# A Mamba block and a mixture of experts on one core: buffers, PSUM banks and an order of their own for the last group's eight expert pairs

## The chip, the cores and the metric

The kernel runs on one core of one Trainium2 chip. The metric is the device time of one execution in microseconds (us). Engines: PE (TensorE), DVE (VectorE), ACT (ScalarE), POOL (GpSimd), and SP, which here only issues DMAs ("SPq" in the trace).

## The reference, cut to what matters

All 32 sequences ("batches" below) of 512 tokens x 256 features, in float32:

```
h = x + mamba(layernorm(x))                      # scan over time, 512 channels x 16 states
x = layernorm(x + h + mlp(layernorm(h)))         # exact gelu
scores = softmax(x @ gate_w.T); top 2 of 8 experts per token
routed = sum over the two: weight * down_e(silu(gate_e(x)) * up_e(x))
shared = down_s(silu(gate_s(x)) * up_s(x))
out = layernorm(x + routed + shared)
```

## The kernel before, in words

**Batches.** Everything up to the routing is done batch by batch. DVE's time scan (`hs`, L1076) is done 64 times a batch; around it ACT forms decays (L655), POOL products `dBx` (L504), PE turns the states (L840) and DVE sums them (L1092).

**Groups.** Batches are collected in groups of 6, 6, 6, 6, 4, 2, 1 and 1. POOL scatters each token's row to two slots of `X_slots` in HBM (L536), sorted by expert. When a group's last batch is routed, DVE computes a table (`where`, `ends`; L1244 to L1273, semaphore `s_meta`): for every tile of 128 slots its first row and its expert. SP writes 128 rows of zeros behind each expert's rows (L406, "pads"), and then the tiles are worked on in pairs.

**A pair** `p` uses `xin[p % 2]`, `wx[p % 2]`, one `xsT`, one `ge` and one PSUM bank `psE`: SP loads two tiles of rows and their weights (L413 `wx`, L415 `xin`); PE transposes (L979, called T here); ACT copies to `xsT` (L739); PE multiplies by gate and up weights (L997, U); ACT tanh (L744), DVE twice (L1222, L1225) to `ge`; PE multiplies by down weights (L1012, D); ACT scales (L755, semaphore `s_yo`); SP stores to `Y_slots` (L431). T of pair p waits for `s_yo` of pair p-1, since `psE` is shared. The last group has eight pairs, 152 to 159.

**Finish.** For each batch f: SP loads `fx` (L444) after batch f-1 is stored, POOL adds the two gathered rows per token (L557, eight DMAs), DVE takes statistics (L1286), POOL the scale, ACT normalizes (L768) and stores `out`. There is one `fx`.

**Order.** Each engine's program is woven from strands (`scan`, `post`, `experts`, `results`, `finish`, ...). Each strand yields at its steps, and the table `AT` gives each step a due time in ticks (64 ticks a batch period); `weave` takes the earliest. Nothing is decided at run time: an engine's queue is this order, and each instruction waits on its semaphores with all behind it. `pairs_in` and `fins_in` say which pairs and finishes fall into which period.

Of the kernel before, what the change touches and what calls it, by code (L numbers as in the profile page):

```python
# [9 lines left out]
def group_sizes(n):  # L10
# [6 lines left out]
    while n:  # L17
# [21 lines left out]
    "ACT_weigh": [7.57, 8.5, 10.26, 11.55, 34.88, 35.01, 35.8, 36.57],  # L39
    "DVE_experts": [124.69, 126.85, 133.73, 139.5, 146.19, 149.9, 150.86, 154.7, 160.93, 165.34, 170.46, 174.99],  # L40
    "DVE_finish": [151.17, 151.17, 151.21, 152.66, 153.77, 171.26, 171.26, 171.41, 171.42, 171.42, 192.14, 192.26,
        193.44, 193.44, 193.44],
    "DVE_meta": [109.64, 109.93, 112.83, 112.83],
    "DVE_post": [59.72, 61.22, 67.08, 70.22, 72.85, 74.06, 75.11, 78.75, 84.22, 84.22, 85.78, 85.78, 85.78, 92.6,
        95.36, 97.26, 97.42, 98.01, 101.51, 103.99, 104.19, 104.25, 104.43, 105.16, 106.33, 108.33, 109.14, 109.14,
        109.97],
    "DVE_pre": [-60.86, -60.52, -60.52, -60.52, -45.76, -29.96, -29.11, -29, -28.49, -24.62, -24.37, -24.22, -22.6,
        -19.43, -18.25, -18.25, -18.11, -17.83, -17.83, -17.74, -17.48],
    "DVE_scan": [1.57, 2.09, 2.09, 2.36, 7.61, 7.63, 9.59, 9.96, 10.13, 11.26, 14.4, 15.73, 17.79, 19.19, 19.19,
# [4 lines left out]
    "DVE_weigh": [15.65, 17.23, 19.8, 20.31, 22.03, 22.04, 22.04, 22.04, 22.25, 22.25, 22.91, 23.69, 24.75, 24.95,  # L54
# [3 lines left out]
    "PE_experts": [123.37, 123.37, 126.75, 127.73, 131.97, 132.13, 138.88, 139.03, 140.94, 140.94, 146.68, 147.27,  # L58
        148.29, 148.29, 153.4, 153.97, 160.38, 160.38, 162.99, 163.09, 168.17, 168.35, 170.23, 170.23],
# [20 lines left out]
        62.82],  # L80
    "SP_B_rows": [-10.64],
    "SP_B_spread": [-7.66, -2.43, -1.84, 1.33, 4.3, 11.62, 24.83, 28.97, 32.58, 35.25, 35.45, 35.45, 43.34, 43.34,
        43.34, 43.34],
    "SP_behind": [0.69, 52.08, 55.74],
    "SP_experts": [110.32, 115.22, 124.29, 133.31, 141.52, 144.6, 147.29, 149.91, 155.71, 164.08, 168.27, 171.3],
    "SP_finish": [137.9, 162.22, 173.84],
# [23 lines left out]
def build(nc, a, out):  # L110
# [62 lines left out]
    with ctx:  # L173
# [1164 lines left out]
```

## Time and profile before

| | |
|---|---|
| median of 3 runs | 5640.32 us (5627.19 to 5643.27) |
| profiled execution | 5645.75 us, span 5644.0 us |
| busy share of the span | DVE 83%, PE 77%, POOL 64%, ACT 57% |
| granted PE clock, mean | 0.896 of full |

Busy shares are averages over a long part in which all engines work and an end in which few do. DVE's tenths in 40 slices of 141 us each read 8 and more up to slice 38, and 2 and 0 in the last two.

### The profile page before, as it was taken

The numbers are of one execution on the slowest core, as the hardware profiler recorded it, in microseconds if no ns is written. First come the engines' busy times: TensorE is split into PE (matmuls) and PEld (weight loads), VectorE is DVE, ScalarE is ACT, GpSimd is POOL, SyncE is SP. The second block draws the span as 40 slices with busy tenths as digits, with TensorE's granted clock in tenths as the row PEclk, the third lists the DMA queues.
The fourth block names the chain that finished last, engine by engine and source line by source line (L and its number), as shares of the span: only waits on it lengthen the run. The fifth ranks groups of instructions, "written<-read, shape, count | busy, mean of one in ns | idle before, by whom it ended". The sixth has DMA issues, their size and how long they took to land. (4 is left out here: it accounts for less than half of the span.)

```text
span 5644.0 us, 75862 instructions
## 1 busy us (share of the span) xinstructions
PE 4329.5 (77%) x20928; PEld 2991.4 (53%) x20928; DVE 4657.8 (83%) x7212; ACT 3195.6 (57%) x5088; POOL 3587.7 (64%) x2252
## 2 busy tenths in 40 slices
PE   4777777788778777777787887777788888887763
PEld 2454445555555555555555555555555555655542
DVE  6888888888888898888888888988988898888820
ACT  4555555555555556556665665665666565565521
POOL 4566666556555567666666766666677775777732
PEclk7888888898889999999999999999999999998885
DMA  1422222233333323332232333223244442555553
GB/s 62 107 78 79 77 72 75 75 105 104 113 113 95 114 85 98 95 101 87 80 91 77 102 93 101 86 76 97 77 120 122 121 116 81 146 151 138 156 136 94
DMA packets 357156, 563.53 MB, mean 100 GB/s; under 512 B 40433, under 2 KB 203378, under 8 KB 356610
## 3 DMA queue, kind: packets, MB, share of 16 engines
q1 hardware_dynamic: 253250, 398.07, 23.4%
q0 software_dynamic: 49152, 67.27, 5.8%
q10 hardware_dynamic: 54336, 93.34, 5.0%
q8 instruction: 174, 2.85, 0.2%
q14 instruction: 244, 2.00, 0.1%
HBM read 440.66 MB, written 186.05 MB: 111 GB/s over the span
## 5 line engine op out<-in xcount | busy, mean ns | idle before, releaser
L504 POOL TENSOR_TENSOR dBx<-dtx,Bbc 128x1024 f32<-128x1024 f32 x1024 | 2441.6, 2415 | 1011.4 <-DVE hs L1076 911.7
L1076 DVE TENSOR_TENSOR_SCAN hs<-ps,dBx 128x512 f32<-128x512 f32 x2048 | 2403.5, 1207 | 192.6 <-ACT ps L655 133.4
L655 ACT ACTIVATE ps<-dt,A 128x512 f32<-128x512 f32 x2048 | 1393.0, 690 | 829.8 <-DVE hs L1076 712.1
L840 PE MATMUL ps<-ident,hs 128*128 128x128 f32 x8192 | 1335.8, 303 | 418.3 <-DVE acc L1092 224.9
L840 PEld LDWEIGHTS ps<-ident,hs 128*128 128x128 f32 x8192 | 1030.3, 155 | 833.0 <-DVE acc L1092 456.5
L1092 DVE SCALAR_TENSOR_TENSOR acc<-ps,C_tok,acc 128x512 f32<-128x512 f32 x1792 | 1288.4, 739 | 191.1 <-PE ps L840 168.8
L805 PE MATMUL ps<-xnT,w_in 128*128 128x512 f32 x512 | 360.0, 842 | 273.4 <-DVE xc L1066 170.3
L557 POOL DMA_INDIRECT fx<-Y_slots,slots x256 | 405.2, 1583 | 210.1 <-DMA fx<-shared 131.4
L536 POOL DMA_INDIRECT X_slots<-xs,slots x256 | 256.6, 1002 | 385.3 <-DVE slots L1210 317.4
L1061 DVE SCALAR_TENSOR_TENSOR xc<-ps,conv_w,xc 128x511 f32<-128x511 f32 (+2 forms) x384 | 286.3, 746 | 178.0 <-ACT xc L615 170.9
L997 PE MATMUL ps<-xsT,wx 128*128 128x128 f32 x2560 | 353.2, 294 | 61.3 <-ACT xsT L739 61.3
L997 PEld LDWEIGHTS ps<-xsT,wx 128*128 128x128 f32 x2560 | 331.4, 207 | 94.0 <-issue 92.1
L805 PEld LDWEIGHTS ps<-xnT,w_in 128*128 128x128 f32 x512 | 118.6, 251 | 393.4 <-issue 306.1
L615 ACT ACTIVATE xc<-ps,conv_b,conv_w 128x512 f32<-128x512 f32 x128 | 99.4, 777 | 398.0 <-PE ps L805 385.7
L857 PE MATMUL ps<-xnT,w_in 128*128 128x512 f32 x512 | 275.6, 642 | 50.2 <-DVE post_tmp L1125 50.2
L1222 DVE SCALAR_TENSOR_TENSOR ge<-ge,ps 128x256 f32<-128x256 f32 x160 | 66.1, 413 | 248.7 <-ACT ge L744 248.4
L921 PE MATMUL ps<-w_m,post_tmp 128*128 128x256 f32 x1024 | 255.5, 380 | 0.0
L887 PE MATMUL ps<-w_out,xc 128*128 128x256 f32 x1024 | 255.3, 384 | 0.0
L904 PE MATMUL ps<-mT,w_m 128*128 128x512 f32 x512 | 237.5, 597 | 2.5 <-ACT mT L695 2.5
L739 ACT ACTIVATE xsT<-ps 128x512 f32<-128x512 f32 x160 | 95.3, 596 | 252.4 <-PE ps L979 237.9
L1012 PE MATMUL ps<-wx,ge 128*128 128x256 f32 x640 | 191.4, 426 | 46.3 <-DVE ge L1225 45.1
L979 PE MATMUL ps<-ident,xin 128*128 128x128 f32 x640 | 107.8, 295 | 152.7 <-DMA xin<-X_slots 144.4
(166 smaller groups left out, 6113.3 us busy)
## 6 DMA issues: line engine op xcount, KB each, us to landing
Bbc<-B_scratch SPq DMA_DIRECT2D x512, 256.0 KB
wx<-in_experts SPq DMA_DIRECT2D x320, 384.0 KB
Y_slots<-zeros ACTq DMA_DIRECT2D x228, 256.0 KB
xin<-X_slots SPq DMA_DIRECT2D x320, 128.5 KB
Y_slots<-xin SPq DMA_DIRECT2D x320, 128.0 KB
xt<-in_x SPq DMA_DIRECT2D x32, 512.0 KB, 5.4
shared<-xt ACTq DMA_DIRECT2D x32, 512.0 KB
fx<-shared SPq DMA_DIRECT2D x32, 512.0 KB, 3.6
```

The source lines that it names most:

```text
L504: pool.tensor_tensor(dBx[u % 3][:], dtx[b % 2][:, 2 * h:2 * h + 2, :], Bbc[g % NBB][:, n % CH:n % CH + 1, :].broadcast_to([P, 2, T]), ALU. ...
L536: pool.indirect_dma_start(out=X_slots[g % 2], out_offset=bass.IndirectOffsetOnAxis(ap=slots[:, b % NKEPT, c, t:t + 1], axis=0), in_=xs[:, ...
L557: pool.indirect_dma_start(out=fx[:, t, :], out_offset=None, in_=Y_slots[g % 2], in_offset=bass.IndirectOffsetOnAxis(ap=slots[:, f % NKEPT, ...
L655: act.activation(psA[s % 2][:], dt[b % 2][:, j, :], ACT.Exp, scale=A[:, j, n:n + 1]).then_inc(s_dA, 1)
L805: i = pe.matmul(bank(b, j)[:], w_in[:, k, j * P:(j + 1) * P], xn[:, k, :], start=(k == 0), stop=(k == KD - 1))
L840: i = pe.transpose(psH[w % 2][:, j * P:(j + 1) * P], hs[(n * CT + j) % NHB][:, t * P:(t + 1) * P], ident[:])
L857: i = pe.matmul(psG[j % 2][:], w_in[:, k, DI + j * P:DI + (j + 1) * P], xn[:, k, :], start=(k == 0), stop=(k == KD - 1))
L921: i = pe.matmul(psG[q][:, t * D:(t + 1) * D], post_tmp[:, k, (2 * q + t) * P:(2 * q + t + 1) * P], w_m2[:, k, :], start=False, stop=(k == ...
L997: i = pe.matmul(psE[:, o * HALF + m * P:o * HALF + (m + 1) * P], w[:, m, (2 * k + o) * P:(2 * k + o + 1) * P], xsT[:, (m * KD + k) * P:(m ...
L1061: dve.scalar_tensor_tensor(out=c[:, j, s:], in0=bank(b, j)[:, 0:T - s], scalar=conv_w[:, j, NK - 1 - s:NK - s], in1=c[:, j, s:], op0=ALU.m ...
L1076: dve.tensor_tensor_scan(hs[s % NHB][:], psA[s % 2][:], dBx[s // 2 % 3][:, s % 2, :], 0.0, ALU.mult, ALU.add).then_inc(s_scan, 1)
L1092: dve.scalar_tensor_tensor(out=o, in0=psH[w % 2][:], scalar=C_tok[b % 2][:, t, n:n + 1], in1=o, op0=ALU.mult, op1=ALU.add).then_inc(s_weig ...
```

## The change

The eight pairs of the last group leave the strands `experts` and `results` and get a strand `last` on each of SP, PE, ACT and DVE, placed at the end of period 31. They use eight weight tiles, eight row tiles, eight `xsT`, and eight halves of `Bbc` as `ge`, all laid over buffers that the scan has left, and six PSUM banks in turn. On PE the steps of three pairs alternate: D of pair q-2, U of pair q-1, T of pair q. SP issues the pads as soon as the table is there, without waiting for the scatter, then all weights, then all rows, then all stores. The function `pad` is also used for the other groups, where `all_rows` follows at once. `fins_in` no longer counts the last group by its pairs. The table `AT` has new numbers for nearly every entry of all strands; one line of it stands at the diff's end. In the diff the first `last` is SP's and the second PE's; ACT's has the same order of steps, and DVE's goes pair by pair. The lines of POOL are from its `finish`.

```diff
-        g = sum(first[g] + groups[g] - 1 <= b for g in range(NG))
+        g = min(sum(first[g] + groups[g] - 1 <= b for g in range(NG)), NG - 1)
         waiting = pairs_to[g - 1] - ended
-        left = groups[g] - (b - first[g] + 1) if g < NG else 1
+        left = max(groups[g] - (b - first[g] + 1), 1)
         take = min(waiting, PAIRS_MAX, -(-waiting // left))
-        ready = sum(groups[g] for g in range(NG) if pairs_to[g] <= ended)
+        ready = sum(groups[g] for g in range(NG - 1) if pairs_to[g] <= ended) + (groups[NG - 1] if b >= NB else 0)
...
+    P0, NLAST = pairs_to[NG - 2], tiles[NG - 1] // 2
...
+        wx_last = [wx[P0 % 2], wx[(P0 + 1) % 2]] + [pair_of(v[:]) for v in (dt[0], dt[1], dtx[0], dtx[1], xc[o], acc[z])]
+        xin_last = [xin[P0 % 2], xin[(P0 + 1) % 2]] + [rows_of(v[:]) for v in (*dBx, xnT[o], xt[NB % NX_IN], xt[(NB + 1) % NX_IN])]
+        xsT_last, ge_last = hs[0:NLAST], [Bbc[q // 2][:, 0, q % 2 * HALF:(q % 2 + 1) * HALF] for q in range(NLAST)]
+        ps_last = [psE, psP, *psA, *psH]
...
+            def pad(g):
+                sp.wait_ge(s_meta, (g + 1) * NMETA)
...
+                for e in range(NE):
+                    r = sp.value_load(ends[g % 2][0:1, e:e + 1], min_val=0, max_val=ROWS - P)
+                    sp.dma_start(X_slots[g % 2][bass.ds(r, P), :], zeros[:, 0:ROW]).then_inc(s_padded[g % 2], 16)
+
+            def all_rows(g):
+                sp.wait_ge(s_scattered, (first[g] + groups[g]) * 2 * NTB * 16)
+                sp.wait_ge(s_padded[g % 2], (g // 2 + 1) * NE * 16)
+
+            def last():
+                g, b = NG - 1, NB - 1
+                for q in range(NLAST):
+                    yield b
+                    if q == 0:
+                        pad(g)
+                        sp.wait_ge(s_scan, NB * STEPS)
+                        sp.wait_ge(s_y_turned, NB * CT)
+                    if q < 2:
+                        sp.wait_ge(s_down_e, P0 - 1 + q)
+                    for i in range(2):
+                        e = sp.value_load(where[g % 2][0:1, 1, 2 * q + i:2 * q + i + 1], min_val=0, max_val=NE * P)
+                        sp.dma_start(wx_last[q][:, i, :], a["experts"].rearrange("e p f -> (e p) f")[
+                            bass.ds(e, P), :]).then_inc(s_wx_last[q], 16)
+                for q in range(NLAST):
+                    yield b
+                    if q == 0:
+                        all_rows(g)
+                        sp.wait_ge(s_kept, (NB - 1) * 16)
+                    if q < 2:
+                        sp.wait_ge(s_Y_out[(P0 + q) % 2], stores(P0 - 2 + q, (P0 + q) % 2))
+                    for i in range(2):
+                        r = sp.value_load(where[g % 2][0:1, 0, 2 * q + i:2 * q + i + 1], min_val=0, max_val=ROWS - P)
+                        sp.dma_start(xin_last[q][:, i, :], X_slots[g % 2][bass.ds(r, P), :]).then_inc(s_xin_last[q], 16)
+                for q in range(NLAST):
+                    yield b
...
+                    sp.wait_ge(s_yo_last, (q + 1) * 2)
...
+                        sp.dma_start(Y_slots[g % 2][bass.ds(r, P), :], xin_last[q][:, i, 0:D]).then_inc(s_Y_last, 16)
...
+            def last():
+                for s_ in range(NLAST + 2):
+                    for q, step in ((s_ - 2, 2), (s_ - 1, 1), (s_, 0)):
+                        if not 0 <= q < NLAST:
+                            continue
+                        bank_, w = ps_last[q % NPS], wx_last[q]
+                        yield NB - 1
+                        if step == 0:
...
+                            if q >= NPS:
+                                pe.wait_ge(s_yo_last, (q - NPS + 1) * 2)
+                            pe.wait_ge(s_xin_last[q], 32)
...
+                            i.then_inc(s_turned_last, 1)
+                        elif step == 1:
+                            pe.wait_ge(s_wx_last[q], 32)
+                            pe.wait_ge(s_xsT_last, q + 1)
...
+                            i.then_inc(s_up_last, 1)
+                        else:
+                            pe.wait_ge(s_hidden_last, q + 1)
...
+                            i.then_inc(s_down_last, 1)
...
                                 if (c, t) == (0, 0):
                                     pool.wait_ge(s_fx_in, 16 * (f + 1))
-                                    for k in range(2):
-                                        pool.wait_ge(s_Y_out[k], stores(pairs_to[g] - 1, k))
+                                    if g == NG - 1:
+                                        pool.wait_ge(s_Y_last, NLAST * 32)
+                                    else:
+                                        for k in range(2):
+                                            pool.wait_ge(s_Y_out[k], stores(pairs_to[g] - 1, k))
...
-    "DVE_weigh": [15.65, 17.23, 19.8, 20.31, 22.03, 22.04, 22.04, 22.04, 22.25, 22.25, 22.91, 23.69, 24.75, 24.95,
+    "DVE_weigh": [15.5, 17.23, 21.12, 21.12, 21.68, 21.68, 22.06, 22.22, 22.66, 22.81, 22.91, 23.41, 24.71, 24.91,
```

SP's queue at the end of the program, before: from the last group's last pad to its first row load. `TENSOR_LOAD` and `ISA` are the reads of the table.

```order
L406 DMA X_slots1<-zeros 128x257
L411 TENSOR_LOAD where1
L411 ISA x2
L412 TENSOR_LOAD where1
L412 ISA x2
L413 ISA
L413 DMA wx0<-in_experts 128x768
L415 ISA
L415 DMA xin0<-X_slots1 128x257
```

The same place after the change:

```order
L426 DMA X_slots1<-zeros 128x257
L444 TENSOR_LOAD where1
L444 ISA x2
L445 ISA
L445 DMA wx0<-in_experts 128x768
L444 TENSOR_LOAD where1
L444 ISA x2
L445 ISA
L445 DMA wx0<-in_experts 128x768
```

Behind the pads a weight load was followed by its row load; now it is followed by the next weight load, and fourteen more, before the first row load. And further down in the same queue, at the rows of the last group's third and fourth pair (`dBx0` and `dBx1` lie under them), after the change:

```order
L456 DMA dBx0<-X_slots1 128x257
L455 TENSOR_LOAD where1
L455 ISA x2
L456 ISA
L456 DMA dBx0<-X_slots1 128x257
L514 DMA fx<-shared 128x1024
L455 TENSOR_LOAD where1
L455 ISA x2
L456 ISA
L456 DMA dBx1<-X_slots1 128x257
```

Batch 30's `fx` load stands between the third and the fourth pair's rows, as it did before, but the stores of the first two pairs, which stood ahead of it, now stand behind all row loads.

PE's queue at the last group, before:

```order
L979 MATMUL ps5<-ident,xin0 128x128 x4
L997 MATMUL ps5<-xsT,wx0 128x128 x8
L1012 MATMUL ps5<-wx0,ge 128x256 x2
L979 MATMUL ps5<-ident,xin1 128x128 x4
L997 MATMUL ps5<-xsT,wx1 128x128 x8
L1012 MATMUL ps5<-wx1,ge 128x256 x2
```

PE's queue at the same place, after (T L1128, U L1137, D L1145; the `hs` tiles are `xsT`, the `Bbc` tiles `ge`):

```order
L1128 MATMUL ps5<-ident,xin0 128x128 x4
L1137 MATMUL ps5<-hs0,wx0 128x128 x8
L1128 MATMUL ps4<-ident,xin1 128x128 x4
L1145 MATMUL ps5<-wx0,Bbc0 128x256 x2
L1137 MATMUL ps4<-hs1,wx1 128x128 x8
L1128 MATMUL ps0<-ident,dBx0 128x128 x4
L1145 MATMUL ps4<-wx1,Bbc0 128x256 x2
L1137 MATMUL ps0<-hs2,dt0 128x128 x8
```

Between U and D of one pair there is now T of the next, and T of a pair stands two places ahead of its U.

On DVE the statistics of batch 29 (L1429 after the change) stand ahead of the first pair's step and those of batch 30 between the seventh pair's and the eighth's; on ACT batch 30's normalizing stands ahead of the eighth pair's tanh.

DVE's queue in the middle of the program (batch 15, `hs` the scan, `acc` the sums), before:

```order
L1092 SCALAR_TENSOR_TENSOR acc1<-ps3,C_tok1,acc1 128x512
L1076 SCALAR_TENSOR_TENSOR hs4<-ps0,dBx2 128x512
L1092 SCALAR_TENSOR_TENSOR acc1<-ps2,C_tok1,acc1 128x512
L1092 SCALAR_TENSOR_TENSOR acc1<-ps3,C_tok1,acc1 128x512
L1076 SCALAR_TENSOR_TENSOR hs5<-ps1,dBx2 128x512
L1076 SCALAR_TENSOR_TENSOR hs6<-ps0,dBx0 128x512
L1076 SCALAR_TENSOR_TENSOR hs7<-ps1,dBx0 128x512
```

The same place after:

```order
L1225 SCALAR_TENSOR_TENSOR acc1<-ps3,C_tok1,acc1 128x512
L1209 SCALAR_TENSOR_TENSOR hs4<-ps0,dBx2 128x512
L1225 SCALAR_TENSOR_TENSOR acc1<-ps2,C_tok1,acc1 128x512
L1209 SCALAR_TENSOR_TENSOR hs5<-ps1,dBx2 128x512
L1225 SCALAR_TENSOR_TENSOR acc1<-ps3,C_tok1,acc1 128x512
L1209 SCALAR_TENSOR_TENSOR hs6<-ps0,dBx0 128x512
L1209 SCALAR_TENSOR_TENSOR hs7<-ps1,dBx0 128x512
```

The second and third sum of the piece stood together, and now a scan step stands between them; in most places of the long part the two orders differ by as little.

## Rows read from the trace of the kernel before

**Rows 1.** Busy time by stretch, the long part: start:end, length, engines, clock, DMA share, GB/s.

```profile
core 0: us, PE busy (x) PEld busy (x) DVE busy (x) ACT busy (x) POOL busy (x), PEclk, DMA share, GB/s
500.00:5300.00 4800.00, 3821.03 (x18765) 2647.02 (x18765) 4159.24 (x6325) 2852.33 (x4544) 3179.27 (x1942) 0.92 0.34 100
5200.00:5250.00 50.00, 44.31 (x269) 35.57 (x270) 40.49 (x60) 30.31 (x53) 32.24 (x21) 1.00 0.65 177
```

**Rows 2.** Shares kept, one a batch (L727), and the two most frequent kinds of wait, 500 to 5300.

```profile
L727 ACTq DMA_DIRECT2D shared<-xt x32: 326/331/366, 324.7 to 5469.7; - x32
...
POOL dBx L504 <- DVE hs L1076: 798.2, 330, 10.6
...
DVE acc L1092 <- PE ps L840: 153.0, 250, 3.7
```

**Rows 3.** Busy time by stretch of 10 us in the end, columns as above.

```profile
5460.00:5470.00 10.00, 5.58 (x28) 3.90 (x26) 7.55 (x33) 3.88 (x8) 6.09 (x8) 1.00 0.22 79
5480.00:5490.00 10.00, 0.00 (x0) 0.00 (x0) 0.00 (x0) 0.00 (x0) 4.77 (x4) 0.50 0.80 144
5490.00:5500.00 10.00, 0.00 (x0) 0.00 (x0) 0.00 (x0) 0.00 (x0) 6.06 (x4) 0.50 0.78 175
5500.00:5510.00 10.00, 6.95 (x24) 5.38 (x24) 0.84 (x2) 1.15 (x3) 0.00 (x0) 0.50 0.32 103
5560.00:5570.00 10.00, 6.20 (x25) 5.11 (x26) 2.53 (x10) 1.82 (x4) 0.47 (x2) 0.67 0.34 108
```

**Rows 4.** Instructions in order of time, SP's DMAs at the last group's start.

```profile
5470.43 0.21 DVE L1273 SCALAR_TENSOR_TENSOR where<-few 1x56 int32<-1x56 f32 x1
...
5470.72 0.38 ACTq L771 DMA_DIRECT2D out<-fx  x1
...
5473.99 0.33 SPq L444 DMA_DIRECT2D fx<-shared  x1
...
5478.28 1.63 POOL L557 DMA_INDIRECT fx<-Y_slots,slots  x1 [2.43 <-DMA fx<-shared]
5479.56 9.82 SPq L406 DMA_DIRECT2D X_slots<-zeros  x8
...
5489.87 1.54 POOL L557 DMA_INDIRECT fx<-Y_slots,slots  x1 [4.41 <-DMA fx<-Y_slots,slots]
...
5493.40 0.36 SPq L413 DMA_DIRECT2D wx<-in_experts  x1
...
5495.43 1.55 POOL L557 DMA_INDIRECT fx<-Y_slots,slots  x1 [0.30 <-issue]
5495.61 0.33 SPq L413 DMA_DIRECT2D wx<-in_experts  x1
5496.13 0.33 SPq L415 DMA_DIRECT2D xin<-X_slots  x1
...
5500.69 1.12 PE L979 MATMUL ps<-ident,xin 128*128 128x128 f32 x4 [31.66 <-DMA xin<-X_slots]
```

**Rows 5.** The last pair, in order of time: T, xsT, U, D, scaling, then batch 31's load.

```profile
5599.67 1.09 PE L979 MATMUL ps<-ident,xin 128*128 128x128 f32 x4 [1.02 <-ACT xin L755]
...
5601.53 3.75 PE L997 MATMUL ps<-xsT,wx 128*128 128x128 f32 x16 [0.78 <-ACT xsT L739]
...
5606.68 2.08 PE L1012 MATMUL ps<-wx,ge 128*128 128x256 f32 x4 [1.39 <-DVE ge L1225]
5608.79 0.84 ACT L755 ACTIVATE xin<-ps,xin 128x256 f32<-128x256 f32 x2 [3.08 <-PE ps L1012]
5611.89 0.37 SPq L444 DMA_DIRECT2D fx<-shared  x1
```

**Rows 6.** A pair of the group before, in order of time, PE alone: T, U, D.

```profile
5454.49 0.60 PE L979 MATMUL ps<-ident,xin 128*128 128x128 f32 x4
5455.86 2.02 PE L997 MATMUL ps<-xsT,wx 128*128 128x128 f32 x16 [0.78 <-ACT xsT L739]
5459.27 1.13 PE L1012 MATMUL ps<-wx,ge 128*128 128x256 f32 x4 [1.38 <-DVE ge L1225]
```

**Rows 7.** Batch 29's finish, in order of time: statistics, normalizing, store.

```profile
5517.68 1.40 DVE L1286 BATCH_NORM_STATS2 stats_fin<-fx 128x6 f32<-128x256 f32 x4
...
5521.57 2.07 ACT L768 ACTIVATE fx<-fx,nb_fin,rs_fin 128x256 f32<-128x256 f32 x4 [0.80 <-POOL nb_fin L570]
5523.67 0.38 ACTq L771 DMA_DIRECT2D out<-fx  x1
```

**Rows 8.** The page, DMA queues: packets, MB, share of 16 engines over the span.

```profile
q1 hardware_dynamic: 253250, 398.07, 23.4%
```

More of the change, by code:

```diff
@@ new lines @@
+    "POOL_pre": [-47.46, 1.12, 3.62],
+    "POOL_scan": [1.53, 3.89, 8.19, 8.19, 8.84, 8.84, 12.39, 14.56, 17.84, 21.37, 24.69, 24.69, 26.76, 29.36, 29.36,
+        29.75, 30.39, 30.39, 31.18, 32.15, 32.15, 32.65, 32.65, 37.83, 42.18, 44.28, 44.81, 45.74, 55.56, 55.72,
+        56.44, 63.18],
+    "SP_B_rows": [-9.09],
+    "SP_B_spread": [-3.46, -2.29, -2.27, 11.26, 17.49, 19.82, 19.82, 19.82, 28.51, 28.51, 28.51, 30.14, 36.45, 39.06,
+        44.23, 44.23],
+    "SP_behind": [27.68, 83.6, 93.32],
@@ L270, in build @@
         s_xin, s_wx, s_Y_out = [[sem(f"{n}{i}") for i in range(2)] for n in ("xin", "wx", "Y_out")]
+        s_wx_last, s_xin_last = [[sem(f"{n}_last{q}") for q in range(NLAST)] for n in ("wx", "xin")]
+        s_Y_last = sem("Y_last")
         s_B_in = [sem(f"B_in{i}") for i in range(NBB)]
@@ L300, in build @@
                                                                             "down_e")]
+        s_turned_last, s_xsT_last, s_up_last, s_tanh_last = [sem(n + "_last") for n in ("turned", "xsT", "up", "tanh")]
+        s_silu_last, s_hidden_last, s_down_last, s_yo_last = [sem(n + "_last") for n in ("silu", "hidden", "down", "yo")]
         NROUTE, NMETA = 21, 18
@@ new lines, in all_rows @@
+            def all_rows(g):
[27 more added lines that the diff above has]
+                    yield b
+                    if q == 0:
+                        sp.wait_ge(s_gathered, gathers(first[before[g]] + groups[before[g]] - 1))
+                    sp.wait_ge(s_yo_last, (q + 1) * 2)
+                    for i in range(2):
+                        r = sp.value_load(where[g % 2][0:1, 0, 2 * q + i:2 * q + i + 1], min_val=0, max_val=ROWS - P)
+                        sp.dma_start(Y_slots[g % 2][bass.ds(r, P), :], xin_last[q][:, i, 0:D]).then_inc(s_Y_last, 16)
@@ L396, in experts @@
                         yield b
-                        sp.wait_ge(s_meta, (g + 1) * NMETA)
-                        sp.wait_ge(s_scattered, (first[g] + groups[g]) * 2 * NTB * 16)
                         if tile == 0:
-                            if g < 2:
-                                sp.wait_ge(s_Y_cleared[g], CLEARS * 16)
-                                sp.wait_ge(s_zeros, 16)
-                                sp.wait_ge(s_behind, 32)
-                            for e in range(NE):
-                                r = sp.value_load(ends[g % 2][0:1, e:e + 1], min_val=0, max_val=ROWS - P)
-                                sp.dma_start(X_slots[g % 2][bass.ds(r, P), :], zeros[:, 0:ROW]).then_inc(s_padded[g % 2], 16)
-                            sp.wait_ge(s_padded[g % 2], (g // 2 + 1) * NE * 16)
+                            pad(g)
+                            all_rows(g)
                         if p >= 2:
@@ L447, in _ @@
                   (experts(), AT["SP_experts"]),
-                  (results(), AT["SP_results"]), (finish(), AT["SP_finish"]))
+                  (results(), AT["SP_results"]), (finish(), AT["SP_finish"]), (last(), AT["SP_last"]))
             sp.wait_ge(s_stored, 16 * NB)
@@ L774, in _ @@
                   (post(), AT["ACT_post"]), (experts(), AT["ACT_experts"]), (results(), AT["ACT_results"]),
-                  (finish(), AT["ACT_finish"]), (clear(), AT["ACT_clear"]))
+                  (finish(), AT["ACT_finish"]), (clear(), AT["ACT_clear"]), (last(), AT["ACT_last"]))
             act.wait_ge(s_stored, 16 * NB)
@@ L1016, in _ @@
             weave((turn(), AT["PE_turn"]), (pre(), AT["PE_pre"]), (post(), AT["PE_post"]), (inputs(), AT["PE_inputs"]),
-                  (experts(), AT["PE_experts"]), (results(), AT["PE_results"]))
+                  (experts(), AT["PE_experts"]), (results(), AT["PE_results"]), (last(), AT["PE_last"]))
         @block.vector
@@ L1225, in experts, with last @@
                         dve.tensor_tensor(ge[:], ge[:], psE[:, HALF:T], ALU.mult).then_inc(s_hidden_e, 1)
+            def last():
+                for q in range(NLAST):
+                    bank_ = ps_last[q % NPS]
+                    yield NB - 1
+                    dve.wait_ge(s_tanh_last, q + 1)
+                    dve.scalar_tensor_tensor(out=ge_last[q], in0=ge_last[q], scalar=1.0, in1=bank_[:, 0:HALF], op0=ALU.add,
+                                             op1=ALU.mult).then_inc(s_silu_last, 1)
+                    dve.wait_ge(s_silu_last, q + 1)
+                    dve.tensor_tensor(ge_last[q], ge_last[q], bank_[:, HALF:T], ALU.mult).then_inc(s_hidden_last, 1)
             def meta():
```

148 lines of the change are left out of this document (97 added, 51 removed), and 30 rows, old and new, of the table AT.

## The prediction

> **What bounds the kernel now.** I read the busy time by stretch first. From 500 to 5300 us DVE is busy 4159 of 4800 us, 87%, and PE 80% [rows 1]: both hold each other up, and a batch takes (5469.7 - 324.7) / 31 = 166.0 us [rows 2]. The reader should see that this part is one thing and the end another. From 5470 on the stretches are nearly empty: PE does nothing from 5480 to 5500, DVE under 1 us in the 10 us after [rows 3]. So the last 170 us are bound by a chain of waits, and that is where the change works.
>
> The instructions in order of time show that chain. The table is there at 5470.6 (5470.43 + 0.21), the pads are issued from 5479.56 to 5489.38, the first weights at 5493.40, and PE starts T of the first pair at 5500.69, having waited 31.66 us [rows 4]. The last pair's scaling ends at 5608.79 + 0.84 = 5609.6 [rows 5]. The eight pairs thus take 5609.6 - 5500.7 = 108.9 us, 13.6 each. A pair alone is 5609.6 - 5599.7 = 9.9 us [rows 5]; the rest is waiting for loads that may only be issued when the stores of the pair two before have landed, because there are two sets of tiles. Behind the last pair come stores, batch 31's load, gathers and normalizing: 5644.0 - 5609.6 = 34.4 us.
>
> **The change part by part.** I follow the same chain with the new queues.
>
> *Start of SP's work.* The pads no longer wait for the scatter but stand behind batch 29's `fx` load, which goes out at 5473.99, 3.3 us after batch 28's store was issued at 5470.72 [rows 4]. On ACT that store now stands ahead of the second half of the shared expert's last copy, which I estimate at 1.9 us earlier (three steps of 0.6 us): `fx` at 5472.1, and the first pad a table read behind it at 5473.2. The eight pads span 9.8 us [rows 4], so they end at 5483.
>
> *Sixteen weight loads.* One tile's two table reads and two issues took 5495.61 - 5493.40 = 2.2 us [rows 4], so 1.1 us each: sixteen take 17.6 us, and the first row load would go out at 5502. But the transfers are 16 x 128 x 768 x 4 bytes = 6.29 MB. SP's and ACT's queue q1 moved 398.07 MB in 23.4% of the span, which is 398.07 / (0.234 x 5644) = 301 GB/s at full share [rows 8]; at some 270, since gathers run beside it, the weights take 23.3 us and are in at about 5508. The rows queue behind. A row load took 5500.69 - 5496.13 = 4.6 us to T with traffic around it [rows 4]. I take T of the first pair at **5511**. Bounds: 5506 if only the issues count (two row issues and 2 to 3 us of landing), and 5531 if the rate is the 144 GB/s of 5480 to 5490 [rows 3], where 6.29 MB take 44 us. I am near the first because that row is full of small packets of gathers and weights are long ones. Against before this is +10.3 us: the early pads win 6 us, and fourteen weight loads ahead of the first rows lose more.
>
> The Trainium skill, "DMA: Bandwidth & Descriptors", section "Queues, rings and completion order", says that each DMA engine consumes one issuer's descriptors in ring order and takes turns between issuers packet by packet. By that rule the first rows do wait for all weights, which speaks against the change and for 5511 rather than 5506; the sum would be 5 us lower without it.
>
> *The pairs.* In the new order D of pair q-2, U of q-1, T of q follow each other on PE. From U's end to D's start are 1.39 us (tanh, two DVE steps) [rows 5], and T of the next pair lies within. The `xsT` copy lies beside D, the scaling beside U, the loads are ahead. What repeats is U + 1.39 + D. At half clock that is 3.75 + 1.39 + 2.08 = 7.22 us [rows 5]; at full clock 2.02 + 1.38 + 1.13 = 4.53 us [rows 6].
>
> Which clock? It stood at 1.00 up to 5470 and at 0.50, that is 1.2 GHz, from 5480 on, after PE had gone idle; with 6.95 busy of 10 us and holes between pairs it stayed at 0.50; in one stretch, with 6.20, it was 0.67 on average, so it rose and fell again [rows 3]. Where PE was busy 44.3 of 50 us it was 1.00 [rows 1]. In the new order PE is busy 6.9 of 7.22 us at half clock, and (0.60 + 2.02 + 1.13) / 4.53 = 83% at full clock, which is closer to the second of these. I take two pairs at half clock and six at full.
>
> The Trainium skill, "TensorE: Matmul & The Clock Gate", Part 1, says the same in general: half rate is the default and sustained activity releases it. By that rule the sum is the one I take; by the half-clock rows around the place it would be 13 us more.
>
> Sum: T and `xsT` of the first pair 1.09 + 0.78 = 1.9; two pairs 14.4; six pairs 27.2; last scaling 0.9; together 44.4 us.
>
> *Batch 30's finish* now stands in the middle of it: its statistics come before the eighth pair's DVE steps, and ACT's normalizing before the eighth tanh. From statistics to the end of normalizing took 5521.57 + 2.07 - 5517.68 = 6.0 us [rows 7]. In that time D and U of the full-clock pairs take 3.2 us, so the eighth tanh is 2.8 us late. Pair block: **47.2 us**, from 5511 to 5558.2.
>
> *Two waits hidden.* SP's queue holds batch 30's `fx` load between the third and fourth pair's rows, until batch 29 is stored. Its gathers ran from 5478.28 to 5497 with 4.4 us of waiting between the halves [rows 4]; landing (4), statistics and normalizing (6.0) and the store (3.3) give about 5509, and 5517 if the weights' traffic doubles the landing times. T of the fourth pair is due at 5511 + 1.9 + 14.4 + 2.0 = 5529, and needs its rows issued by 5524. So the wait is covered by 7 to 15 us; beyond that it costs its own length. The sixteen stores go at 1.1 us each, 2.2 a pair against 4.5, so SP keeps up. Batch 30 itself: load 4, gathers 15 + 4.4 + 4, ready at 5536 to 5544; its statistics are due at 5549. Hidden.
>
> *The end* behind the last scaling keeps its shape: 34.4 us.
>
> *The new order table* in the long part: the same work, in places one instruction earlier or later. DVE is idle 13% of 166 us, so there is something to win or lose. One typical wait of DVE is 153.0 / 250 = 0.6 us [rows 2]. One more or one less a batch is 0.6 x 31 = 19 us. I take 0, since nothing in the orders favours a side.
>
> Sum in the profile's time: +10.3 (start) + 47.2 - 108.9 (pairs) = -51.4; span 5644.0 - 51.4 = 5592.6, and the execution 5645.75 - 51.4 = 5594.4. The profiled execution is 5.4 us above the median of the runs, so I say **5589 us**.
>
> **The rivals.**
> 1. *The clock stays at half.* For it: it did so in every pair from 5500 to 5560 [rows 3]. Against: those had holes. Six periods cost 2.69 us more, less the 2.8 us that batch 30 then no longer costs: +13, 5602 us.
> 2. *The weights come slowly*, at 144 GB/s [rows 3]: T at 5531, +20, 5609 us.
> 3. *SP stands at batch 30's load.* If batch 29's gathers, statistics or store are late beyond 5524, the fourth pair's rows are late by as much. With 10 us, 5599 us.
> 4. *The new order costs more than the end gives* (the other side). The mechanism: POOL may write `dBx` only when DVE's scan has used it, a wait of 798.2 / 330 = 2.4 us on average [rows 2]; if the new order adds one a batch that DVE then feels, that is 75 us: 5664 us, slower. It decides from 51.4 / 31 = 1.7 us a batch on. For it: nearly every due time changed, in queues without slack. Against: in the orders neighbours swap places, no more.
>
> **How the numbers follow.** A change within 0.3% (17 us) can't be told from none: the limits are 5623 and 5657. Forecast 0.48, clock 0.17, weights 0.12, SP 0.07, new order 0.16. Faster: the first four, 0.84, less a little of their overlap with small losses in the long part, 0.83. Of the fourth rival's 0.16, 0.10 lie within the limits (1.1 to 2.2 us a batch) and 0.07, with what was taken off, above. The range: from 5589 down 19 (one wait less a batch) and 5 (issue-bound start), 5565; up 13 (clock) and 19 (one wait more), 5621, which takes in rivals 1 to 3 and leaves out rival 4. Rounded outward: 5563 to 5622.
>
> **What would show it.** T of the first pair some 40 us after batch 28's store, later than before by 10; PE's D, U, T with no hole but 1.4 us, the granted clock at 1.00 from the third pair on; the last scaling 34 us ahead of the end; 166.0 us a batch unchanged. It would be wrong if a batch's time moved by 1 us, if PE's waits at the rows came back behind the `fx` load, or if PE waited for weights.

## The result and the profile after

| | before | after |
|---|---|---|
| median | 5639.85 us (4 runs, 5627.19 to 5643.27) | 5446.44 us (4 runs, 5429.85 to 5454.42) |
| profiled execution, span | 5645.75, 5644.0 us | 5454.42, 5452.7 us |
| first and last share copy | 324.7, 5469.7 us | 316.7, 5335.8 us |
| a batch between them | 166.0 us | 161.9 us |
| last share copy to the end | 174.3 us | 116.9 us |

The ratio is 0.9657, with a 95% interval of 0.9627 to 0.9687: 193 us faster, where 51 were forecast. The busy time of the engines is nearly what it was, on a shorter span. Part 1 of the changed kernel's page:

```profile
PE 4290.8 (79%) x20928; PEld 2976.0 (55%) x20928; DVE 4632.5 (85%) x7212; ACT 3190.3 (59%) x5088; POOL 3587.7 (66%) x2252
```

The line with one entry a batch, the copies into `shared`, cuts the time in two, and that cut is the main reading of this case. In the columns of [rows 2]:

```profile
L800 ACTq DMA_DIRECT2D shared<-xt x32: 326/331/366, 316.7 to 5335.8; - x32
```

From the first copy to the last are 31 batches: (5335.8 - 316.7) / 31 = 161.9 us against 166.0. The first copy itself comes 8.0 us earlier. So the last copy comes 133.9 us earlier than before, and the end behind it is 174.3 - 116.9 = 57.4 us shorter. 133.9 + 57.4 = 191.3, which is the difference of the spans. The end is where the prediction looked; the long part was taken at nothing. The long part by stretch, in the columns of [rows 1]:

```profile
500.00:5300.00 4800.00, 3904.73 (x19256) 2720.82 (x19254) 4196.02 (x6458) 2881.76 (x4613) 3232.72 (x1989) 0.91 0.36 104
```

DVE is busy 4196 of 4800 us, 87.4% against 86.7%. Between the first copy and the last, DVE's waits for other engines fall from 21.6 to 18.3 us a batch and its busy time from 142.1 to 141.3 us. The shorter batch is thus in the main less waiting between the same instructions.

**The end**, in stretches of 10 us, answers to [rows 3]:

```profile
5350.00:5360.00 10.00, 0.00 (x0) 0.00 (x0) 0.00 (x0) 0.00 (x0) 3.56 (x3) 0.50 0.99 300
5360.00:5370.00 10.00, 0.00 (x0) 0.00 (x0) 0.52 (x2) 0.00 (x0) 3.07 (x2) 0.50 1.07 325
5370.00:5380.00 10.00, 4.32 (x19) 3.98 (x20) 1.27 (x7) 2.67 (x5) 1.71 (x4) 0.50 0.69 238
5380.00:5390.00 10.00, 7.94 (x55) 7.00 (x54) 2.11 (x5) 4.44 (x10) 6.32 (x4) 0.95 0.79 183
5390.00:5400.00 10.00, 7.60 (x52) 6.85 (x53) 2.11 (x5) 3.83 (x9) 6.21 (x4) 1.00 0.71 156
```

The weights move at 300 and 325 GB/s (all the core's transfers together, batch 29's gathers among them) with PE idle. PE starts in the stretch from 5370, and the clock is at 0.95 in the next and at 1.00 in the one behind it. The instructions in order of time, answering to [rows 4]:

```profile
5338.75 10.17 SPq L426 DMA_DIRECT2D X_slots<-zeros  x8
...
5349.81 3.67 SPq L445 DMA_DIRECT2D wx<-in_experts  x4
...
5365.43 1.42 SPq L445 DMA_DIRECT2D acc<-in_experts  x2
5367.74 3.97 SPq L456 DMA_DIRECT2D xin<-X_slots  x4
...
5374.90 1.09 PE L1128 MATMUL ps<-ident,xin 128*128 128x128 f32 x4 [39.77 <-DMA xin<-X_slots]
...
5378.46 0.33 SPq L514 DMA_DIRECT2D fx<-shared  x1
```

The pads start 3.0 us behind the last share copy (5335.80), where they were 9.9 behind it before; the sixteen weight loads take from 5349.81 to 5366.85, the first rows go out at 5367.74, and T is at 5374.90. The `fx` load of batch 30 waits until 5378.46 between the third and the fourth pair's rows, and PE has no wait on it. The same view a little later shows D (L1145) of two pairs in a row, and then the eighth pair's tanh, D and scaling behind batch 30's normalizing:

```profile
5386.20 1.13 PE L1145 MATMUL ps<-wx,Bbc 128*128 128x256 f32 x4 [0.95 <-DVE Bbc L1368]
...
5390.50 1.13 PE L1145 MATMUL ps<-dt,Bbc 128*128 128x256 f32 x4 [0.95 <-DVE Bbc L1368]
...
5411.47 2.07 ACT L863 ACTIVATE fx<-fx,nb_fin,rs_fin 128x256 f32<-128x256 f32 x4 [1.76 <-POOL nb_fin L643]
...
5414.00 0.38 ACT L845 ACTIVATE Bbc<-ps 128x256 f32<-128x256 f32 x1 [0.46 <-ACT fx L863]
...
5415.34 2.07 PE L1145 MATMUL ps<-acc,Bbc 128*128 128x256 f32 x4 [4.73 <-DVE Bbc L1368]
5417.46 0.84 ACT L850 ACTIVATE xt<-ps,xt 128x256 f32<-128x256 f32 x2 [3.08 <-PE ps L1145]
```

D to D is 5390.50 - 5386.20 = 4.30 us, with the next pair's U and the one's after it T between them. The eighth tanh (L845) comes at 5414.00, behind the normalizing (L863). PE has idled 4.73 us by the eighth D, which then takes 2.07 us instead of 1.13, the half-clock duration [rows 5]. Behind the same hole it took 1.47 us in the experiment late_pads below.

### The profile page after: what moved, and what is told of

It reads as the page before. It is cut to its first block and busy times, and to the rows that moved or that the text cites. A ratio compares the mean times of both kernels' runs of the same rounds, so it can differ in the third digit from the quotient of the medians.

```text
span 5452.7 us, 75679 instructions
## 1 busy us (share of the span) xinstructions
PE 4290.8 (79%) x20928; PEld 2976.0 (55%) x20928; DVE 4632.5 (85%) x7212; ACT 3190.3 (59%) x5088; POOL 3587.7 (66%) x2252
## 3 DMA queue, kind: packets, MB, share of 16 engines
q1 hardware_dynamic: 253250, 398.07, 24.2%
## 5 line engine op out<-in xcount | busy, mean ns | idle before, releaser
L935 PE MATMUL ps<-ident,hs 128*128 128x128 f32 x8192 | 1350.3, 305 | 486.2 <-DVE acc L1225 285.5
L900 PE MATMUL ps<-xnT,w_in 128*128 128x512 f32 x512 | 324.9, 762 | 178.8 <-DVE xc L1199 170.3
L1092 PE MATMUL ps<-xsT,wx 128*128 128x128 f32 x2432 | 318.6, 286 | 39.0 <-ACT xsT L812 38.7
L1092 PEld LDWEIGHTS ps<-xsT,wx 128*128 128x128 f32 x2432 | 303.3, 201 | 74.7 <-issue 74.2
L952 PE MATMUL ps<-xnT,w_in 128*128 128x512 f32 x512 | 279.2, 685 | 0.0
L900 PEld LDWEIGHTS ps<-xnT,w_in 128*128 128x128 f32 x512 | 108.9, 235 | 271.5 <-issue 267.7
L812 ACT ACTIVATE xsT<-ps 128x512 f32<-128x512 f32 x152 | 90.0, 592 | 212.8 <-PE ps L1074 211.8
L1107 PE MATMUL ps<-wx,ge 128*128 128x256 f32 x608 | 176.7, 416 | 45.6 <-DVE ge L1358 42.9
L1016 PEld LDWEIGHTS ps<-w_m,post_tmp 128*128 128x128 f32 x1024 | 189.8, 190 | 36.7 <-issue 14.4
L982 PEld LDWEIGHTS ps<-w_out,xc 128*128 128x128 f32 x1024 | 193.2, 190 | 25.6
```

Source lines behind the costliest of these rows:

```text
L900: i = pe.matmul(bank(b, j)[:], w_in[:, k, j * P:(j + 1) * P], xn[:, k, :], start=(k == 0), stop=(k == KD - 1))
L935: i = pe.transpose(psH[w % 2][:, j * P:(j + 1) * P], hs[(n * CT + j) % NHB][:, t * P:(t + 1) * P], ident[:])
L952: i = pe.matmul(psG[j % 2][:], w_in[:, k, DI + j * P:DI + (j + 1) * P], xn[:, k, :], start=(k == 0), stop=(k == KD - 1))
L982: i = pe.matmul(psG[q][:, t * D:(t + 1) * D], c[:, k, (2 * q + t) * P:(2 * q + t + 1) * P], w_out[:, k, :], start=False, stop=(k == CT - 1))
L1016: i = pe.matmul(psG[q][:, t * D:(t + 1) * D], post_tmp[:, k, (2 * q + t) * P:(2 * q + t + 1) * P], w_m2[:, k, :], start=False, stop=(k == ...
L1092: i = pe.matmul(psE[:, o * HALF + m * P:o * HALF + (m + 1) * P], w[:, m, (2 * k + o) * P:(2 * k + o + 1) * P], xsT[:, (m * KD + k) * P:(m ...
```

## The experiments

Fifteen further kernels were built from the two: the same code with other due times, or one edit of the last group's strand. Besides the ratio, each row gives the two parts from its profiled execution. The kernel before ran beside each of them, with medians of 5625.6 to 5642.5 us; gains and losses in us below are against the one beside the kernel. Since the kernels ran in several rounds, two of them are compared by their ratios and not by their medians. The two parts rest on one execution each. How much they vary without a cause can be seen in the long part: after, seq_last, late_pads and rows_early have the same code and order there, and their last share copies come at 5335.8, 5315.9, 5334.0 and 5309.2 us.

| kernel | median us | ratio to before, 95% | a batch | end part |
|---|---|---|---|---|
| code_only | 5575.7 | 0.988 (0.9849 to 0.991) | 165.6 | 118.7 |
| table_only | 5515.9 | 0.9792 (0.9763 to 0.9821) | 161.8 | 174.2 |
| new_act | 5578.0 | 0.989 (0.9855 to 0.9925) | 164.2 | 170.2 |
| new_pe | 5761.8 | 1.0214 (1.0185 to 1.0243) | 169.8 | 175.0 |
| act_pe | 5639.8 | 0.9995 (0.997 to 1.002) | 165.3 | 170.7 |
| act_dve | 5684.0 | 1.0101 (1.008 to 1.0122) | 167.9 | 167.3 |
| act_pe_dve | 5497.1 | 0.9779 (0.9758 to 0.98) | 161.4 | 170.5 |
| old_sp | 5481.7 | 0.9744 (0.9726 to 0.9763) | 161.1 | 174.0 |
| pre_act | 5636.8 | 1.0018 (0.9998 to 1.0039) | 165.5 | 173.4 |
| act_notpre | 5874.7 | 1.0436 (1.0406 to 1.0466) | 173.3 | 171.5 |
| seq_last | 5449.1 | 0.9667 (0.9639 to 0.9695) | 161.3 | 127.9 |
| late_pads | 5448.0 | 0.9657 (0.9632 to 0.9682) | 161.7 | 121.7 |
| rows_early | 5430.3 | 0.9629 (0.9599 to 0.966) | 161.0 | 115.4 |
| after_old_sp | 5419.7 | 0.9617 (0.9593 to 0.9641) | 161.0 | 115.8 |
| best | 5401.9 | 0.959 (0.9568 to 0.9612) | 160.5 | 112.0 |

### Code and table apart

code_only is the changed code with the old numbers for all 32 old strands; the strands `last` keep theirs, ACT's 0.75 later (134.91 for 134.16, and so on). The edit of one old strand:

```diff
-    "SP_behind": [27.68, 83.6, 93.32],
+    "SP_behind": [0.69, 52.08, 55.74],
...
```

> The new code of the last group with the old order table (ACT's steps of the new strand 0.75 tick later, so that batch 29's normalizing still stands ahead of them). Theory A, the gain has two sources, the end (57 us from batch 31's last share copy to the end: 174.3 before, 116.9 after) and the order table (134 us ahead of it): about 5640 - 57 = 5583 us, a batch at 166.0 us. Theory B, the table matters only together with the code (the function pad, the finishes that no longer count the last group): near 5446 us, a batch at 162 us.

table_only is the old code with the new numbers.

> The old code with the new order table. Theory A: 5640 - 134 = 5506 us, a batch at 161.9 us, the end as before (174 us). Theory B: near 5640 us.

Theory A held on both sides: 5575.7 and 5515.9 us, and the product of the ratios, 0.988 x 0.9792 = 0.9675, is the change's 0.9657 within the intervals. The code acts on the end part alone (118.7 us; a batch 165.6 against 166.0, the last copy 12 us earlier, inside the spread above), the table on the batches alone (161.8 us, end 174.2).

### Which engine's order

Each engine's queue depends only on its own engine's numbers, so the table can be divided by engine without any other effect. In these the old code got new numbers for all strands of the engines named. One strand's first line, for new_pe:

```diff
-    "PE_turn": [4.33, 4.9, 8.45, 9.97, 12.05, 12.46, 12.62, 13.39, 19.52, 19.52, 19.73, 20.13, 20.28, 20.28, 21.11,
+    "PE_turn": [4.62, 5.23, 8.11, 8.57, 12.27, 12.27, 12.73, 13.29, 19.39, 19.64, 19.73, 20.13, 20.28, 20.28, 21.11,
...
```

> The old code with the new order on PE alone. Theory A1, the gain is in the input convolution (DVE's waits for ACT's first tap fell from 143 to 58 us, ACT's waits for PE's input product from 349 to 220 us) and comes from PE's order, which brings those products earlier: 5510 to 5570 us. Theory A2, it comes from DVE's order, which puts the taps later: 5625 to 5655 us here.

> The old code with the new order on ACT alone. Theory A1 (PE's order) and A2 (DVE's order) both: 5620 to 5655 us. Theory A3, ACT's order lets the first tap go out earlier: 5510 to 5590 us.

> The old code with the new order on ACT and DVE. With ACT's alone DVE's waits for ACT's decays rose from 103 to 172 us; with all engines they are 77 us. Theory C1, DVE's new order takes those waits back: 5515 to 5545 us. Rival C2, DVE's order fits PE's new one only (PE's alone cost 119 us): slower than 5578 us.

> The old code with the new order on ACT and PE. So far: ACT alone 65 us faster, PE alone 119 slower, ACT and DVE 58 slower, all three 128 faster. Theory D1, the three orders are one schedule, and any two of them make the third wait: slower than 5640 us, with DVE's waits for PE's second MLP product (143 us with PE alone, 21 with all three) at 100 us or more. Rival D2, ACT's and PE's orders are the gain and DVE's is neutral: 5500 to 5530 us.

> The old code with the new order on ACT, PE and DVE, but POOL's and SP's as before. Theory C1 and C2 both: most of the 127 us, 5515 to 5535 us. Rival C3, the rest of the gain lies with the loads of Bbc and with POOL (POOL's waits for Bbc fell from 89 to 27 us): 5550 us or more.

ACT alone gains 65 us (A3's range), PE alone loses 119 (A1 and A2 are out), ACT with PE is nothing (D2 is out, and D1 too: the kernel was not slower, and the wait for the second MLP product, 100 us or more by D1, was 0.3 us), ACT with DVE loses 58 (C1 is out, C2 foretold it), and the three together gain 128 (C3 is out; the others' range is missed by 18 us on the fast side). What stands is C2: DVE's new order fits PE's. Beside ACT's alone it costs 123 us (from 65 gained to 58 lost), beside ACT's and PE's it brings 128. DVE alone and PE with DVE were not tried. So the gain belongs to no engine. The simplest view is DVE's waits in the first five batches after the first share copy, which hold no expert pairs. Before (us in total, times, longest):

```profile
DVE xc L1061 <- ACT xc L615: 24.8, 15, 3.1
DVE acc L1092 <- PE ps L840: 24.0, 41, 2.5
DVE hs L1076 <- ACT ps L655: 16.0, 15, 1.7
```

With the three new orders (other line numbers for the same instructions; L1027 is the first tap, L1042 the scan, L1058 the sum):

```profile
DVE acc L1058 <- PE ps L806: 18.6, 46, 1.3
DVE hs L1042 <- ACT ps L621: 12.1, 10, 1.5
DVE xc L1027 <- ACT xc L581: 10.5, 11, 1.7
```

All of DVE's waits there are 15.6 us a batch before and 9.7 after, and a batch is 156.0 and 150.0 us: the same 6 us. Over all 31 batches, with the whole new table (table_only), DVE's waits fall from 21.6 to 18.1 us a batch and its busy time from 142.1 to 141.3, together what a batch gained (166.0 to 161.8). In the first five batches with PE's new order alone they are 17.8, and a batch is 157.7:

```profile
DVE acc L1058 <- PE ps L806: 26.0, 46, 1.9
DVE stats_post L1068 <- PE ps L887: 25.3, 5, 5.6
...
DVE xc L1027 <- ACT xc L581: 13.9, 10, 2.1
```

The taps' wait fell here as well, but a wait that did not exist before stands beside it: `stats_post` (L1102 before), 25.3 us in five batches, for PE's second MLP product. By the numbers of the table, one more group of the scan's transposes stands ahead of the last of these products in PE's new order, and in DVE's new order one more sum stands ahead of the statistics that need it. With all three new orders the wait is gone in these batches. But it is gone with ACT's and PE's alone too, where DVE's order is the old one, and there another has grown, the scan's for PE (3.3 us before):

```profile
DVE acc L1058 <- PE ps L806: 23.6, 40, 1.8
DVE hs L1042 <- PE ps L806: 20.7, 10, 2.1
```

That is the coupling: a step moved on one engine saves a wait and makes another, and which one is made depends on the orders of two other engines. Which moves in the table bring the gain is not shown.

The same is seen inside one engine:

> The old code and order, with the new due times of ACT's strand pre alone (normalizing, first taps, tanh, the dt steps). With ACT's whole new order the kernel took 5578 us against 5643, and DVE's waits for ACT's first tap fell from 143 to 55 us. Theory A3, the moved taps are the source: 5570 to 5590 us, the waits for the tap as low. Rival, it is the places of ACT's scan steps and its other strands around the taps: 5630 to 5650 us.

> The old code and order, with the new due times of ACT's strands except pre. All of ACT's new due times gave 65 us, pre's alone nothing, although its waits for the tap fell. Theory M1, the gain of ACT's order is in its scan, post and expert steps: 5570 to 5590 us. Rival M2, it needs both parts: 5625 to 5650 us.

A3 fell with pre_act (5636.8 us, in its rival's range). M1 fell with act_notpre, and M2 was right that both parts are needed but missed the size: `pre` alone gives nothing and the rest of ACT alone costs 241 us (173.3 us a batch), yet the two together give 65. I had read the fall of one row as the cause. From 500 to 5300 us, before and then with ACT's new `pre`:

```profile
DVE xc L1061 <- ACT xc L615: 143.1, 83, 3.4
DVE hs L1076 <- ACT ps L655: 102.9, 106, 4.1
DVE ge L1222 <- ACT ge L744: 84.3, 53, 8.9
```

```profile
DVE acc L1058 <- PE ps L806: 188.5, 262, 3.7
DVE hs L1042 <- ACT ps L621: 130.7, 201, 3.9
DVE ge L1188 <- ACT ge L710: 97.7, 75, 8.1
DVE xc L1027 <- ACT xc L581: 60.3, 54, 3.1
```

The taps' wait (L1061, now L1027) falls from 143.1 to 60.3 us, and three others rise: sums 153.0 [rows 2] to 188.5, scan 102.9 to 130.7, `ge` 84.3 to 97.7. All of DVE's waits are 21.6 us a batch before and 21.2 with the new `pre`. The wait moved.

> The old code with the new order on all engines but SP, to be compared with 5516 us (new order on all). Theory C3: the late Bbc loads come back, POOL's waits for them rise from 41 to 80 us or more and the time to 5540 us or more. Theory C1: within 10 us of 5516.

C3 is refuted: the waits for `Bbc` did come back (POOL waited 93 us instead of 41 from 500 to 5300), and the kernel was not slower. The medians differ by 34 us in its favour, but they are of different rounds; by the ratios (0.9744 and 0.9792, intervals that just touch) it is some 27 us, and by the spans of the profiles 22, so C1's "within 10 us" was missed too. In this pair of profiles the last four batches took 170.6 us each against 176.8, which is 25 us. That SP's new order costs was tested again in the changed kernel:

> The changed kernel with the old due times for SP's old strands. With the old code, SP's old order beside the new order of the others took 5482 us against 5516 with all new, and the last four batches 170.6 us each against 176.8. Theory S1, SP's new order alone costs some 20 us: 5420 to 5430 us, the last four batches near 171. Rival S2, that was a difference of two runs of the old code only: 5440 to 5450 us.

```diff
-    "SP_behind": [27.68, 83.6, 93.32],
+    "SP_behind": [0.69, 52.08, 55.74],
...
```

SP's six other old strands got their old numbers in the same way. The median is 5419.7 us, at the edge of S1's range, but the intervals of the two ratios overlap, and part of these 27 us is spread. The last four batches decide it: 169.9 us each here and 169.9 in the kernel best below, with SP's old numbers, against 173.3, 173.5, 174.2 and 172.7 in after, seq_last, late_pads and rows_early, with its new ones. So S1 held in kind. SP's new order costs 3 to 4 us in each of the last four batches, some 14 us in all; the rest of the 27 is not shown to come from it. Which SP strand costs it stays open.

### The end part

```diff
-                for s_ in range(NLAST + 2):
-                    for q, step in ((s_ - 2, 2), (s_ - 1, 1), (s_, 0)):
+                for s_ in range(NLAST):
+                    for q, step in ((s_, 0), (s_, 1), (s_, 2)):
```

> The changed kernel, but on PE and ACT each of the eight pairs is done to its end before the next begins; tiles, banks and loads as changed. Theory T1, what the end gained is mostly that no pair waits for its loads, and the interleaving adds 1.6 us a pair at full clock (5.9 against 4.3): 5446 + 13 = 5459 us. Rival T2, the holes bring the clock back to half, 9.1 us a pair: 5446 + 34 = 5480 us.

By the ratios (0.9667 and 0.9657) the interleaving can't be told from nothing; by the end part of the profiled executions it is 127.9 - 116.9 = 11 us, near T1's 13. The long part was 20 us shorter in this kernel's profile, with the same code and order, so the end part is the sharper measure. The instructions in order of time bear it out: from the first T to the last scaling's end are 5409.44 - 5353.61 = 55.8 us here and 43.4 after the change, 12.4 longer; T came 1.4 us earlier, and behind the last scaling both have 34.4 us. PE alone, one pair and the next T:

```profile
5376.57 0.60 PE L1091 MATMUL ps<-ident,dBx 128*128 128x128 f32 x4
5378.24 2.02 PE L1100 MATMUL ps<-hs,dt 128*128 128x128 f32 x16 [1.07 <-ACT hs L804]
5381.65 1.13 PE L1108 MATMUL ps<-dt,Bbc 128*128 128x256 f32 x4 [1.38 <-DVE Bbc L1331]
5382.61 0.60 PE L1091 MATMUL ps<-ident,dBx 128*128 128x128 f32 x4
```

T to T is 6.04 us at full clock (T1: 5.9). T2 fell: with holes of 1.07 and 1.38 us the clock stays up, at 1.00 from 5370 to 5400.

```diff
                     if q == 0:
+                        sp.wait_ge(s_scattered, (first[g] + groups[g]) * 2 * NTB * 16)
                         pad(g)
```

> The changed kernel, but SP waits for the scatter before the last group's pads, as before. The pads began 4 to 5 us before the scatter landed, and all else on SP stands behind them: T of the first pair 5 us later, 5451 us. Rival: the first rows wait for the weights' transfers, which ran at 300 to 325 GB/s and start as much later, so that it is the same 5 us; if the gathers of batch 29 get through better in the meantime, 5446 us.

The end part grew by 121.7 - 116.9 = 4.8 us, as expected: T came 44.6 us behind the last share copy instead of 39.1, and the pairs took 42.8 us instead of 43.4. The ratios (0.9657 both) can't show it.

```diff
-                for q in range(NLAST):
+                def weights(q):
...
-                for q in range(NLAST):
+                def rows(q):
...
+                yield from weights(0)
+                for q in range(NLAST):
+                    if q + 1 < NLAST:
+                        yield from weights(q + 1)
+                    yield from rows(q)
```

> The changed kernel, but SP issues the weights of two pairs, then the rows of the first, and so on in turn, instead of all sixteen weight loads ahead of the first rows. Theory E1: T of the first pair comes 17 us earlier (at 22 instead of 39 us behind the last share copy), but batch 30's finish, which was ready only 4 us before its place, then sets the end: 5446 - 7 = 5439 us. Rival E2, the end follows the pairs: 5430 us. Rival E3, the transfers are the bound and nothing moves: 5446 us.

The median was 5430.3 us, which is E2's number, but by luck: the end part only went from 116.9 to 115.4 us, where E2 had 16 us less and E1 had 7. The rest is the long part, which has the same code and order as after and was 26.6 us shorter in this profile. T came earlier as said, at 5333.4, 24.2 us behind the share copy (5309.2) instead of 39.1. Then, in order of time:

```profile
5346.10 2.07 ACT L834 ACTIVATE fx<-fx,nb_fin,rs_fin 128x256 f32<-128x256 f32 x4 [36.92 <-POOL nb_fin L614]
...
5348.63 0.60 ACT L812 ACTIVATE hs<-ps 128x512 f32<-128x512 f32 x1 [0.46 <-ACT fx L834]
...
5349.37 3.76 PE L1108 MATMUL ps<-hs,wx 128*128 128x128 f32 x16 [14.87 <-ACT hs L812]
```

U waits 14.87 us, because on ACT the copy to `xsT` (L812) stands behind batch 29's normalizing (L834), which is not ready. E1 is right that the finishes are the bound, but it is batch 29's that meets the pairs first, and it takes nearly all of the gain. The run also shows what the late T was made of: in the changed kernel the first row load went out 31.9 us behind the last share copy, after 17 us of issuing weight loads, and T followed it by 7.2 us (5374.90 - 5367.74); here T followed the first row load by 4.9 us. Of the 14.9 us between the two, 12.6 are thus SP's issuing and 2.3 the way from there to T, which the weights ahead of the rows can have made longer.

```diff
-    "DVE_last": [135.94, 138.39, 138.39, 140.22, 147.13, 147.13, 147.78, 191.48],
+    "DVE_last": [126.0, 126.0, 138.39, 140.22, 147.13, 147.13, 147.78, 191.48],
...
```

> The changed kernel with SP's old due times, the rows issued in turn with the weights, the first pairs' ACT and DVE steps ahead of batch 29's finish, and the eighth tanh ahead of batch 30's normalizing. Theory E1 (the chain of finishes through the one fx tile sets the end once the pairs are early): from the last share copy to the end 111 us against 116.9 after the change, 5446 - 20 - 6 = 5420 us. Rival E2, the pairs set it: the end follows them by their 15 us, 102 us and 5411 us.

E1 held for the end part, 112.0 us against its 111. The total of 5401.9 us, the fastest version, is 18 us below E1's, since the long part was shorter than in the profile of after (last share copy at 5292.7). Besides this edit it has those of rows_early and after_old_sp, and in `ACT_last` 132.0 for its first seven numbers and 156.0 for 164.97. In order of time, batch 30's `fx` load, its statistics and batch 31's load:

```profile
5336.83 0.33 SPq L485 DMA_DIRECT2D fx<-shared  x1
...
5362.25 1.41 DVE L1400 BATCH_NORM_STATS2 stats_fin<-fx 128x6 f32<-128x256 f32 x4 [6.36 <-DMA fx<-Y_slots,slots]
...
5372.35 0.37 SPq L485 DMA_DIRECT2D fx<-shared  x1
```

From load to load through the one `fx` tile are 5372.35 - 5336.83 = 35.5 us, while T of the first pair was at 5316.7, 24.0 us behind the last share copy. The end no longer follows the pairs. They are not wholly out of the chain: batch 29's statistics stand behind the second pair's steps on DVE and began at 5327.86, 12.7 us behind its last gather (5315.14), where in after it was 7.5 (5361.94 to 5369.48). I estimate from this that some 5 of the 112 us still come from the pairs.

## Why the prediction was wrong

**The step that failed** is "*The new order table* in the long part ... I take 0, since nothing in the orders favours a side", with its bound of 19 us. The table measured 127 us by itself (table_only), a gain, and the last share copy came 134 us earlier in the profile of the change. Two things were wrong in it. The price of one typical DVE wait (0.6 us) was taken as if at most one wait a batch could change. But DVE had 21.6 us of waits a batch (15.6 in the first five, which have no pairs), and the table took 3.5 of them away (5.8 in the first five); the prediction had this pool before it, as DVE's 13% of idle time, and did not use it as the bound. And the comparison of orders, "neighbours swap places, no more", looked at one engine's queue at a time; whether a swap wins or loses is decided by what the other engines do at that time. The fourth rival had the right scale (a few us in every batch) and the wrong sign, and the wait that it named, POOL's for the scan, fell (798.2 us before, 726.2 after, 500 to 5300). No case of the forecast allowed a gain of more than 19 us from the table. What the runs leave open is which of its 671 changed numbers bring the gain.

**Start of SP's work, weights, first T.** Right in kind: early pads help, weights ahead of the rows cost. From the last share copy T came at 39.1 us; 41.3 was predicted, 31.0 before [rows 4]. The weights moved at 300 to 325 GB/s, where I had worked out 301 from [rows 8] and taken 270, not at the 144 of [rows 3]; rival 2 is out. The first row load went out 31.9 us behind the last share copy (32.3 predicted). Undoing the early pads cost 4.8 us, where I had 6.

**The pairs.** 5418.30 - 5374.90 = 43.4 us, 47.2 predicted, 108.9 before. The clock rose within the first pair (in seq_last within the second), not after two, so rival 1 is out; the repeat is 4.30 us, not 4.53, since D overlaps the next U by 0.16 us and U takes 1.95 us, not 2.02. The trace agrees with the clock rule that I had cited from the Trainium skill, "TensorE: Matmul & The Clock Gate", Part 1: sustained activity brought 1.00. Behind the 4.73 us hole D took its half-clock duration again, 2.07 us.

**Batch 30's finish** delayed the eighth tanh by 3.4 us (2.8 predicted), plus 0.9 for D at half clock, which I had not counted.

**Hidden waits.** Batch 30's `fx` load went out at 5378.46, 42.7 us behind the last share copy (39 to 47 predicted), and cost nothing; rival 3 is out. **The end** is 34.4 us, as predicted.

The end's terms were thus +8.1 - 65.5 = -57.4 us against +10.3 - 61.7 = -51.4. Interleaving is 11 us of what the code gained and the early pads 5. The larger part is in seq_last too, which has neither a hole for loads nor the interleaving: there the eight pairs take 55.8 us against 108.9. Of these 53 us some 20 are the same matmuls at the higher clock (PE is busy 54.5 us in the eight pairs before and 34.1 in seq_last), and the other 33 are waits that are gone, above all those for the loads.

## What to carry to other kernels

When a change carries a new order for all engines, its effect can't be read from one queue or from one row of waits. Look at how much waiting the busiest engine has in a repeated part, take that whole amount as the bound of the gain, and multiply by the repeats. It is a wide bound (21.6 us a batch here, of which 3.5 were won), and it is none for a loss: act_notpre added 7.5 us of waits a batch. Orders of several engines are one schedule; parts of a better one can be worse than either whole. And cut a long profile at a mark that comes once per repeat: it separates an 11 us effect at the end from a spread of over 25 us elsewhere.

## What the runs showed of the hardware

While SP's weight loads of 3072 bytes per partition were under way, beside batch 29's gathers, the core moved 300 to 325 GB/s with a DMA share of 0.99 to 1.07 (after, 5350 to 5370), more than twice the 144 GB/s at a share of 0.80 that gathers and pads gave [rows 3]. SP issued these loads, each with one read of the table, at 1.1 us apiece (sixteen in 17.0 us). PE's clock held at 1.00 with regular holes of 1.1 and 1.4 us in each 6.0 us (seq_last), but in the last group before the change, with holes of 0.8, 1.4 and 1.0 us at half clock in each 10 us and longer ones between pairs, it stayed mostly at 0.50 ([rows 3], [rows 5]).
